# Attention sums stored with channels on partitions, denominators inverted once a head group and multiplied in by the row projection

## The chip, the cores and the metric

The kernel runs on one core of one Trainium2 chip. The metric is the device time of one execution in microseconds. The kernel before takes 2670.48 us, the median of 3 runs (2664.89 to 2671.22). The profiled execution took 2660.48 us, and its trace spans 2658.8 us.

## The reference, cut to what matters

One transformer block on x of shape 4 x 2048 x 256 (B, T, C), in float32. H = 16 heads of DH = 16 channels.

```python
def attention(x):                     # x: the layer-normed input
    q, k, v = heads(x)                # each (b, 16, 2048, 16), latent projections folded in, rotary on half
    scores = einsum('bhqd,bhkd->bhqk', q, k) / sqrt(16)
    att = softmax(where(causal, scores, -inf), axis=-1)
    y = einsum('bhqk,bhkd->bhqd', att, v)
    return y.transpose(0, 2, 1, 3).reshape(b, t, c) @ Wc

x = x + attention(layernorm(x))
z = layernorm(x).reshape(-1, 256)
gate = top-2 of 8 experts by z @ Wr + br, softmax over the two
x = x + sum over experts of gate * (relu(z @ W1 + b1) @ W2 + b2)
```

The softmax's denominator is the same for all 16 channels of a head and query. The kernel computes it as a 17th channel: the values have a column of ones, so the sum of the unnormalised exponentials comes out beside the 16 sums of values.

## The kernel before, in words

Four stages follow each other, each its own block of engine programs: `project` (queries, keys and values, written to HBM), `attend`, `mix` (the output projection Wc, the residual, the layer norm, the routing), and `experts`. The change touches `attend` and `mix`.

**attend** works through NG = 16 groups, a group w being one batch and GH = 4 heads (b = w // 4). Two streams share TensorE (PE):
- the maxima: PE computes scores with queries on partitions (L1004) into one of two PSUM slots `ps_m`, and VectorE (DVE) takes row maxima from it (L888 for whole blocks of keys, L892 on the diagonal). A ring counter (`plan_with_ring`) gives the slots in turn; PE waits for `piece_taken` of two pieces ago. When 12 (or the last 4) query tiles are done, DVE reduces them ("chain", L907), PE turns them ("turn_max", L1011), DVE splits them in two parts (L917, L919), and SyncE's queue (SP) sends them through HBM into the rows of `q_st` (`place_minus`, L733, L739).
- the sums: PE computes scores with keys on partitions (L963), ScalarE (ACT) takes the exponential (L865, L861), GpSimd (POOL) masks the diagonal (L814), and PE sums (L984): four heads, 17 rows each at partitions 32 h, into one PSUM bank `ps_o` of 512 queries.

A group has NSTEP = 40 "sum" steps, one for each tile of 128 keys, in four chunks c of 512 queries: 4, 8, 12 and 16 steps, that is steps 0 to 3, 4 to 11, 12 to 23 and 24 to 39. After the last step of a chunk ACT copies `ps_o` to `out_sb[:, c, :]` (L871). Then comes the operation "turn_out", 64 times in all: PE transposes the four 128 x 128 pieces of `out_sb` into a slot of the `ps_m` ring (L1015), DVE inverts the 16 denominators of each token (L926), waits that the store of two chunks before has landed, and multiplies (L931) into `y_sb`, and SP stores that to `y_dram`, which has tokens as rows (L757). At the end of a group's last sum, SP loads the heads of group w + 3 (`load`: 13 DMAs at L716 and L724, 3.6 MB).

The order of everything in `attend` is written out beforehand by a planner in Python, `attention_plan`. It simulates the engines with fixed durations and picks at each point the ready kind that can start first, less its `HOLD`. Every engine's program goes through the same list PLAN: each of PE, ACT, DVE and SP executes, in that order and with its own waits, what falls to it. So an engine that waits in one entry does nothing of what lies behind it.

**mix** takes NB = 16 blocks of 512 tokens. Before: SP loads a block of `y_dram` (`load_y`, L1136), PE transposes it (`turn_y`, L1452), ACT copies the halves to `yt` (L1206), PE multiplies by Wc (`mix_heads`, L1467), DVE adds the residual (L1328), then follow layer norm, transposes of the normalised rows, the router (L1479), the choice of two experts on DVE, and counts. POOL writes each token's entry into the experts' lists by 128 indirect DMAs, 8 a block (L1189), as soon as DVE has made its slots (L1437). SP also loads x four blocks ahead, stores the rows, and brings in 1 MB of expert weights a block. `experts` starts when POOL's last entry is written. In row p and column j of a block, token 4 p + j is kept.

## Time and profile before

| | us |
|---|---|
| median of 3 runs (lowest, highest) | 2670.48 (2664.89, 2671.22) |
| the profiled execution's own time | 2660.48 |
| its span in the trace | 2658.8 |
| PE busy | 2356.7 (89%) |
| DVE busy | 2044.3 (77%) |
| ACT busy | 1581.8 (59%) |
| POOL busy | 824.5 (31%) |

Busy time is the time in which an engine executed something; for PE the ends are modelled. The share is that of the whole span, so it mixes stages: `attend` runs from about 258 to 1930 us, `mix` to about 2132 us, `experts` to the end. In the rows further down a form such as 128x512 is partitions by elements, "idle before" is time in which the engine did nothing before these instructions, and the name behind an arrow is what ended that time. SPq is the queue of DMA-issuing instructions on SyncE.

### The profile page before, as it was taken

What the parts mean: (1) busy time and instruction counts of PE and PEld (TensorE: products, weight loads), DVE (VectorE), ACT (ScalarE), POOL (GpSimd) and SP (SyncE); (2) the same over time, 40 slices, a digit from 0 to 9 for tenths busy, and PEclk for the clock granted to TensorE, in tenths of its full rate; (3) what the DMA queues carried; (4) which work ended last, traced back from release to release, by engine and by line L of the source; (5) the groups of instructions that cost most, each with busy time, mean ns of one, the idle gap of its engine ahead of it and who ended that gap; (6) DMA issues with size and microseconds to landing.
All of it is one profiled execution on the core that took longest, in us unless ns stands there. A gap on an engine that the chain in (4) does not pass through costs nothing. (4 is left out here: it accounts for less than half of the span.)

```text
span 2658.8 us, 48214 instructions
## 1 busy us (share of the span) xinstructions
PE 2356.7 (89%) x15842; PEld 1342.6 (50%) x15842; DVE 2044.3 (77%) x5000; ACT 1581.8 (59%) x2716; POOL 824.5 (31%) x1132
## 2 busy tenths in 40 slices
PE   6786699999999999999999999998879379999998
PEld 6675233333343333333333333333256168998897
DVE  3785988988989899888889988993068557777776
ACT  3663177776777777766777777777745234444443
POOL 1444021121122112112112112112137755566554
PEclk7998599999999999999999999999989689999999
DMA  3777824135045045044144144101099323333332
GB/s 136 260 267 222 118 45 76 41 60 119 30 63 89 28 65 89 28 64 76 42 63 74 45 65 73 45 8 31 21 296 281 115 89 114 107 105 109 111 110 71
DMA packets 147718, 256.02 MB, mean 96 GB/s; under 512 B 72968, under 2 KB 92042, under 8 KB 139157
## 3 DMA queue, kind: packets, MB, share of 16 engines
q1 hardware_dynamic: 114544, 164.96, 28.0%
q0 software_dynamic: 29904, 80.65, 9.2%
q10 hardware_dynamic: 3028, 7.33, 1.7%
q8 instruction: 135, 2.21, 0.4%
q14 instruction: 107, 0.87, 0.1%
HBM read 147.65 MB, written 107.76 MB: 96 GB/s over the span
## 5 line engine op out<-in xcount | busy, mean ns | idle before, releaser
L865 ACT ACTIVATE prob<-ps_s 128x512 f32<-128x512 f32 (+5 forms) x1620 | 1078.5, 714 | 464.8 <-PE ps_s L963 462.2
L888 DVE TENSOR_REDUCE maxes<-ps_m 128x2 f32<-128x1024 f32 x768 | 914.1, 1222 | 112.6 <-PE ps_m L1004 109.3
L963 PE MATMUL ps_s<-q_st,k_st 50*128 50x512 f32 (+3 forms) x2560 | 605.4, 409 | 78.9 <-ACT prob L865 56.9
L1004 PE MATMUL ps_m<-k_st,q_st 48*128 48x512 f32 (+3 forms) x2560 | 605.1, 444 | 75.2 <-DVE maxes L888 39.6
L814 POOL TENSOR_SCALAR_AFFINE_SELECT prob<-prob 128x256 f32<-128x256 f32 x512 | 203.2, 406 | 1341.8 <-ACT prob L865 1211.9
L984 PE MATMUL ps_o<-prob,v_sb 128*17 128x512 f32 (+3 forms) x5120 | 606.7, 547 | 1.4 <-ACT prob L865 0.7
L1004 PEld LDWEIGHTS ps_m<-k_st,q_st 48*128 48x128 f32 x2560 | 273.6, 192 | 531.2 <-DVE maxes L888 261.3
L892 DVE CUSTOM_DVE_ANT_0 junk<-ps_m,causal 128x128 f32<-128x128 f32 (+3 forms) x1024 | 453.0, 484 | 47.6 <-PE ps_m L1004 45.9
L963 PEld LDWEIGHTS ps_s<-q_st,k_st 50*128 50x128 f32 x2560 | 316.6, 188 | 299.9 <-ACT prob L865 222.0
L1741 ACT ACTIVATE h_hi<-ps_turned 128x512 fp32r<-128x512 f32 x142 | 84.9, 598 | 213.9 <-PE ps_turned L1856 212.4
L94 PE MATMUL ps_out<-experts_hi,h_lo 128*128 (+1 forms) x568 | 171.6, 302 | 0.1
L984 PEld LDWEIGHTS ps_o<-prob,v_sb 128*17 128x17 f32 x5120 | 86.5, 95 | 168.5 <-issue 138.4
L96 PE MATMUL ps_out<-experts_hi,h_hi 128*128 (+1 forms) x568 | 160.4, 282 | 0.0
L95 PE MATMUL ps_out<-experts_lo,h_hi 128*128 (+1 forms) x568 | 160.1, 282 | 0.0
L1189 POOL DMA_INDIRECT list_dram<-entry,slots x128 | 123.9, 968 | 76.2 <-issue 39.6
L1770 DVE TENSOR_TENSOR h<-ps_hidden,b_sb 128x512 f32<-128x512 f32 x142 | 98.3, 692 | 43.9 <-PE ps_hidden L96 43.4
L1784 DVE TENSOR_TENSOR y<-ps_out,b_sb 128x256 f32<-128x256 f32 x142 | 60.3, 425 | 87.0 <-PE ps_out L96 87.0
L94 PE MATMUL ps_hidden<-experts_hi,x_lo 128*128 (+1 forms) x284 | 125.5, 442 | 0.3 <-issue 0.2
L96 PE MATMUL ps_hidden<-experts_hi,x_hi 128*128 (+1 forms) x284 | 112.6, 396 | 0.0
L95 PE MATMUL ps_hidden<-experts_lo,x_hi 128*128 (+1 forms) x284 | 112.4, 396 | 0.0
L1731 ACT ACTIVATE xn<-rows,lists 128x256 f32<-128x256 f32 x142 | 84.0, 591 | 47.1 <-DMA rows<-rows_dram,lists 46.2
L95 PEld LDWEIGHTS ps_out<-experts_lo,h_hi 128*128 128x128 f32 x568 | 107.6, 189 | 0.1
(187 smaller groups left out, 3065.8 us busy)
## 6 DMA issues: line engine op xcount, KB each, us to landing
parts_dram<-parts SPq DMA_DIRECT2D x64, 512.0 KB, 3.8
q_st<-parts_dram SPq DMA_DIRECT2D x84, 256.0 KB, 8.9
k_st<-parts_dram SPq DMA_DIRECT2D x84, 256.0 KB, 18.2
v_dram<-v_out SPq DMA_DIRECT2D x16, 544.0 KB, 5.5
xin<-in_L_attn_x SPq DMA_DIRECT2D x16, 512.0 KB, 6.0
ffn_raw<-in_L_ffn_W POOLq DMA_DIRECT2D x32, 256.0 KB, 5.2
y_dram<-y_sb SPq DMA_DIRECT2D x64, 128.0 KB, 2.0
split_hi<-ffn_hi POOLq DMA_DIRECT2D x16, 512.0 KB, 3.2
```

The lines of the kernel that those rows point to most:

```text
L94: nc.tensor.matmul(out, s_lo, m_hi, start=first, stop=False, skip_group_check=True)
L95: nc.tensor.matmul(out, s_hi, m_lo, start=False, stop=False, skip_group_check=True)
L96: return nc.tensor.matmul(out, s_hi, m_hi, start=False, stop=last, skip_group_check=True)
L814: nc.gpsimd.affine_select(out=tile, in_=tile, compare_op=ALU.is_ge, fill=0.0, base=0, pattern=[[0, 2], [1, P]], channel_multiplier=-1).the ...
L865: last_exp = nc.scalar.activation(prob[:, at:at + n, lo:TB], bank[:, 0:n, lo:TB], ACT.Exp, scale=DH ** -0.5)
L888: return nc.vector.tensor_reduce(maxes[:, 2 * pair:2 * pair + 2, qt, kc], bank[:, :, :], AX.X, ALU.max)
L892: last = nc.vector.tensor_tensor_reduce(junk[:, slot, i, 0:w], bank[:, i, 0:w], causal[:, TB - w:TB], 1.0, NEG, ALU.add, ALU.max, maxes[:, ...
L963: mm = nc.tensor.matmul(ps_s[k % 2][:, i, lo:TB], k_st[half(h % 2, ROWS), w % BUFS, h // 2, kt * P:(kt + 1) * P], q_st[half(h % 2, ROWS), ...
L984: mm = nc.tensor.matmul(ps_o[32 * h:32 * h + VW, lo:TB], v_sb[:, w % BUFS, kt, h, :], prob[:, (s % PROBS) * GH + h, lo:TB], start=STEP_FIR ...
L1004: mm = nc.tensor.matmul(ps_m[slot][:, i, 0:wide], q_st[half(i, STACK), w % BUFS, pair, qt * P:(qt + 1) * P], k_st[half(i, STACK), w % BUFS ...
L1189: pool.indirect_dma_start(list_dram[:, :], bass.IndirectOffsetOnAxis(ap=slots[:, j, i:i + 1], axis=0), entry[:, j, i, :], None).then_inc(s ...
L1770: nc.vector.tensor_tensor(out=h[:, s % 2, :], in0=ps_h[s % 2][:, :], in1=b1_sb[:, bass.ds(e, 1), :].rearrange("p a n -> p (a n)"), op=ALU. ...
```

## The change

At the end of a chunk, SP stores `out_sb[:, c, :]` as it is, 128 partitions by 512 queries, 256 KB, into `y_dram`, which now has 32 rows a head (16 channels, the denominator, 15 unused) and tokens as columns. The 64 "turn_out" operations go, from the planner too. In the next group's steps, SP loads the group's denominators as 128 x 64 (at step 3), DVE inverts them (at step 12), SP stores them to `inverse_dram` (at step 20); the last group's are handled by ACT's queue and DVE at the start of `mix`. There `load_y` brings channels on partitions, `load_inverse` brings each head's inverse 16 times over, DVE multiplies the two into `yt` in the tile order (`scale_heads`), and the transposes and ACT's copies of y go. A constant table in `attend` is made by an iota instead of a load. Cut to its core:

```diff
-HOLD = {"max": -171, "scores": -140, "sum": 0, "turn_out": -266}
+HOLD = {"max": -171, "scores": -140, "sum": 0}
+HEAD_ROWS = 32
+INVERSE_LOAD, INVERSE_MADE, INVERSE_STORE = 3, 12, 20
...
-        if outs:
-            ready["turn_out"] = max(outs[0][1], taken[-SLOTS]) + 53
...
-        else:
-            plan.append(("turn_out", outs.pop(0)[0]))
-            tile_free[:], issued = [start + 430, start + 430], start + 430
-            vector = max(start + 630, vector - 85) + 700
-            taken.append(vector)
...
+        sums_v = y_dram.rearrange("(g r) n -> g r n", r=HEAD_ROWS)
...
+        def load_sums(eng, g, to, done):
+            eng.dma_start(to, sums_v[g % HG * GH:(g % HG + 1) * GH, DH,
+                          g // HG * T:(g // HG + 1) * T].rearrange("g (q n) -> g q n", n=T // HEAD_ROWS)
+                          ).then_inc(done, 16)
+
+        def store_inverse(eng, g, of, done):
+            eng.dma_start(inverse_dram[g % HG * GH:(g % HG + 1) * GH, g // HG * T:(g // HG + 1) * T].rearrange(
+                "g (q n) -> g q n", n=T // HEAD_ROWS), of).then_inc(done, 16)
...
-                elif e[0] == "turn_out":
-                    w, c = e[1] // CH, e[1] % CH
-                    sp.wait_ge(piece_taken, ring + 1)
-                    to = y_dram[(w // HG) * T + c * TB:(w // HG) * T + (c + 1) * TB,
-                                (w % HG) * (GH * DH):(w % HG + 1) * (GH * DH)]
-                    sp.dma_start(to.rearrange("(j p) n -> p j n", p=P),
-                                 y_sb[:, c % 2, :, :, :].rearrange("p j h d -> p j (h d)")
-                                 ).then_inc(y_stored[c % 2], 16)
-                elif e[0] == "sum" and (e[1] + 1) % NSTEP == 0 and (e[1] + 1) // NSTEP + BUFS - 1 < NG:
-
-                    sp.wait_ge(summed, e[1] + 1)
-                    load(sp, (e[1] + 1) // NSTEP + BUFS - 1)
-            for i in range(2):
-                sp.wait_ge(y_stored[i], 16 * (NG * CH // 2))
+                elif e[0] == "sum":
+                    w, c, _ = STEP_LIST[e[1]]
+                    step = e[1] % NSTEP
+                    if w and step == INVERSE_LOAD:
+
+                        for u in range(2):
+                            sp.wait_ge(y_stored[u], 32 * w)
+                        if w >= 3:
+                            sp.wait_ge(inverse_stored[(w - 1) % 2], 16 * ((w - 1) // 2))
+                        load_sums(sp, w - 1, inverse[:, (w - 1) % 2, :], sums_in)
+                    elif w and step == INVERSE_STORE:
+                        sp.wait_ge(inverse_made, w)
+                        store_inverse(sp, w - 1, inverse[:, (w - 1) % 2, :], inverse_stored[(w - 1) % 2])
+                    if STEP_LAST[e[1]]:
+
+                        sp.wait_ge(out_copied, w * CH + c + 1)
+                        sp.dma_start(y_dram[w % HG * P:(w % HG + 1) * P, w // HG * T + c * TB:w // HG * T + (c + 1) * TB],
+                                     out_sb[:, c, :]).then_inc(y_stored[c % 2], 16)
+                    if e[1] + 1 == (w + 1) * NSTEP and w + BUFS < NG:
+
+                        sp.wait_ge(summed, e[1] + 1)
+                        load(sp, w + BUFS)
+            for u in range(2):
+                sp.wait_ge(y_stored[u], 32 * NG)
+                sp.wait_ge(inverse_stored[u], 16 * len(range(u, NG - 1, 2)))
...
+                    w, c, _ = STEP_LIST[e[1]]
+                    if w and c < 2:
+                        act.wait_ge(y_stored[c], 32 * w)
                     act.wait_ge(summed, e[1] + 1)
-                    nc.scalar.copy(out_sb[:, STEP_LIST[e[1]][1], :], ps_o[:, :]).then_inc(out_copied, 1)
+                    nc.scalar.copy(out_sb[:, c, :], ps_o[:, :]).then_inc(out_copied, 1)
...
-                elif e[0] == "turn_out":
-                    c, made = e[1] % 2, e[1] // 2
-                    src = ps_m[slot][:, 0, :].rearrange("p (j h d) -> p j h d", j=TILES, h=GH)
-                    dve.wait_ge(piece_made, ring + 1)
-                    nc.vector.reciprocal(rec[:, c, :, :], src[:, :, :, DH]).then_inc(rec_made, 1)
-                    dve.wait_ge(rec_made, e[1] + 1)
-                    if made:
-
-                        dve.wait_ge(y_stored[c], 16 * made)
-                    nc.vector.tensor_tensor(out=y_sb[:, c, :, :, :], in0=src[:, :, :, 0:DH],
-                                            in1=rec[:, c, :, :].unsqueeze(3).broadcast_to([P, TILES, GH, DH]),
-                                            op=ALU.mult).then_inc(piece_taken, 1)
+                elif e[0] == "sum" and e[1] >= NSTEP and e[1] % NSTEP == INVERSE_MADE:
+                    w = e[1] // NSTEP - 1
+                    dve.wait_ge(sums_in, 16 * (w + 1))
+                    nc.vector.reciprocal(inverse[:, w % 2, :], inverse[:, w % 2, :]).then_inc(inverse_made, 1)
...
-                    else:
-                        pe.wait_ge(out_copied, e[1] + 1)
-                        for j in range(TILES):
-                            mm = nc.tensor.transpose(ps_m[slot][:, 0, j * P:(j + 1) * P],
-                                                     out_sb[:, e[1] % CH, j * P:(j + 1) * P], ident[:, :])
...
             def load_y(n):
-                sp.dma_start(y_in[:, n % YB, :, :], y_v[n, :, :, :]).then_inc(y_loaded[n % YB], 16)
+                tokens = slice(n * TB, (n + 1) * TB)
+                for a in range(CC):
+                    sp.dma_start(y_in[:, n % YB, a, :],
+                                 y_v[a * HP:(a + 1) * HP, 0:DH, tokens]).then_inc(y_loaded[n % YB], 16)
+
+            def load_inverse(n):
+                if n == NB - CH:
+                    sp.wait_ge(inverse_stored[(NG - 1) % 2], 16 * (NG // 2))
+                tokens = slice(n * TB, (n + 1) * TB)
+                for a in range(CC):
+                    sp.dma_start(inverse_in[:, n % 2, a, :],
+                                 inverse_dram[a * HP:(a + 1) * HP, tokens].unsqueeze(1).broadcast_to([HP, DH, TB])
+                                 ).then_inc(y_loaded[n % YB], 16)
...
                 if n + YB < NB:
-                    sp.wait_ge(rows_turned, units(n, False) + 2)
+                    sp.wait_ge(y_scaled, n + 1)
                     load_y(n + YB)
+                if n + 2 < NB:
+                    sp.wait_ge(y_scaled, n + 1)
+                    load_inverse(n + 2)
...
+            act.dma_start(inverse[:, :],
+                          y_v[(HG - 1) * GH:HG * GH, DH, (B - 1) * T:B * T].rearrange(
+                              "g (q n) -> g q n", n=T // HEAD_ROWS)).then_inc(sums_in, 16)
...
-            copy_turned(yt)
             act.wait_ge(weights_in, 3 * 16)
             for n in range(NB + 2):
                 if n == 0:
-                    act.wait_ge(mixed, 2)
-                    copy_turned(yt)
+                    act.wait_ge(inverse_made, NG)
+                    act.dma_start(inverse_dram[(HG - 1) * GH:HG * GH, (B - 1) * T:B * T].rearrange(
+                        "g (q n) -> g q n", n=T // HEAD_ROWS), inverse[:, :]
+                                  ).then_inc(inverse_stored[(NG - 1) % 2], 16)
...
+            def scale_heads(n):
+                dve.wait_ge(y_loaded[n % YB], 32 * CC * (n // YB + 1))
+                if n:
+                    dve.wait_ge(mixed, 2 * n)
+                tt(out=yt[:, :, :, :], in0=y_in[:, n % YB, :, :].rearrange("p a (q j) -> p a j q", j=TILES),
+                   in1=inverse_in[:, n % 2, :, :].rearrange("p a (q j) -> p a j q", j=TILES),
+                   op=ALU.mult).then_inc(y_scaled, 1)
+
+            scale_heads(0)
+            dve.wait_ge(sums_in, 16 * NG)
+            nc.vector.reciprocal(inverse[:, :], inverse[:, :]).then_inc(inverse_made, 1)
+            scale_heads(1)
...
+                if n + 2 < NB:
+                    scale_heads(n + 2)
                 if m >= 0:
...
-            def turn_y(n):
-                pe.wait_ge(y_loaded[n % YB], 16 * (n // YB + 1))
-                turn(y_in[:, n % YB, :, :])
...
-                pe.wait_ge(turned_copied, units(n, False) + 2)
+                pe.wait_ge(y_scaled, n + 1)
...
-                                                yt[:, a, j * P:(j + 1) * P], wc_sb[:, a, :],
+                                                yt[:, a, j, :], wc_sb[:, a, :],
...
-    y_dram = nc.dram_tensor("y_dram", (B * T, C), F32).ap()
+    y_dram = nc.dram_tensor("y_dram", (H * HEAD_ROWS, B * T), F32).ap()
+    inverse_dram = nc.dram_tensor("inverse_dram", (H, B * T), F32).ap()
```

What is left out is declarations, arguments, the semaphores that are passed from `attend` to `mix`, waits whose counts follow from the removed transposes, and the iota.

## Rows read from the trace of the kernel before

**Rows 1.** Windows of attend: start:end, length, busy us by engine, PEclk, DMA share, GB/s.
```profile
400.00:1816.00 1416.00, 1314.67 (x9322) 547.96 (x9324) 1258.11 (x2730) 1024.41 (x1630) 263.22 (x534) 0.98 0.33 59
1816.00:1931.00 115.00, 93.84 (x592) 30.50 (x591) 7.12 (x19) 86.91 (x137) 18.01 (x39) 0.98 0.06 16
```

**Rows 2.** Groups by line, whole span: busy us, mean ns of one, idle before.
```profile
L1015 PE MATMUL ps_m<-ident,out_sb 128*128 128x128 f32 x256 | 42.2, 288 | 9.3 <-DVE maxes L888 4.9 <-DVE maxes L892 1.5 <-ACT out_sb L871 1.4
...
L931 DVE TENSOR_TENSOR y_sb<-ps_m,rec 128x256 f32<-128x256 f32 x64 | 27.2, 424 | 4.7 <-DMA y_dram<-y_sb 2.6
...
L926 DVE RECIPROCAL rec<-ps_m 128x16 f32<-128x16 f32 x64 | 16.2, 254 | 112.0 <-PE ps_m L1015 111.1
```

**Rows 3.** Timeline of PE around one turn_out: start us, us, instruction.
```profile
1093.81 0.66 PE L1015 MATMUL ps_m<-ident,out_sb 128*128 128x128 f32 x4
1094.39 0.53 PE L1004 MATMUL ps_m<-k_st,q_st 48*128 48x512 f32 x2
```

**Rows 4.** Timeline of SP's queue at the start of group 8.
```profile
1131.79 2.83 SPq L716 DMA_DIRECT2D q_st<-parts_dram  x6
...
1138.60 0.43 SPq L733 DMA_DIRECT2D minus_dram<-minus_rows  x1
1161.86 1.23 SPq L739 DMA_DIRECT2D q_st<-minus_dram  x2
```

**Rows 5.** The y_dram store behind the load of 930.14 us: start, and landing.
```profile
L757 SPq DMA_DIRECT2D y_dram<-y_sb x1: 432/432/432, 936.1 to 936.1; - x1
...
DMA to landing us min/median/max: 23.0/23.0/23.0
```

**Rows 6.** Timeline of ACT: group's end and next chunk 1's end, twice.
```profile
426.63 0.59 ACT L871 COPY out_sb<-ps_o 128x512 f32<-128x512 f32 x1
...
457.23 0.59 ACT L871 COPY out_sb<-ps_o 128x512 f32<-128x512 f32 x1
...
1637.58 0.59 ACT L871 COPY out_sb<-ps_o 128x512 f32<-128x512 f32 x1
...
1666.99 0.59 ACT L871 COPY out_sb<-ps_o 128x512 f32<-128x512 f32 x1
```

**Rows 7.** Timeline of DVE and PE around step 12 of group 8.
```profile
1160.56 2.36 DVE L888 TENSOR_REDUCE maxes<-ps_m 128x2 f32<-128x1024 f32 x2 [0.31 <-PE ps_m L1004]
...
1165.24 0.42 DVE L931 TENSOR_TENSOR y_sb<-ps_m,rec 128x256 f32<-128x256 f32 x1 [2.16 <-DMA y_dram<-y_sb]
...
1165.72 0.50 PE L1004 MATMUL ps_m<-k_st,q_st 48*128 48x512 f32 x2 [2.42 <-DVE y_sb L931]
```

**Rows 8.** Timeline of all engines: end of attend, start of mix.
```profile
1925.79 0.58 ACT L871 COPY out_sb<-ps_o 128x512 f32<-128x512 f32 x1 [1.17 <-PE ps_o L984]
...
1927.92 0.36 SPq L757 DMA_DIRECT2D y_dram<-y_sb  x1
1930.35 0.36 ACTq L1199 DMA_DIRECT2D numbers<-in_tile_numbers  x1
```

**Rows 9.** Timeline of POOL in mix: first and last of 128 list writes.
```profile
1966.69 1.05 POOL L1189 DMA_INDIRECT list_dram<-entry,slots  x1 [34.80 <-DVE slots L1437]
...
2130.96 0.97 POOL L1189 DMA_INDIRECT list_dram<-entry,slots  x1 [0.31 <-issue]
```

**Rows 10.** Windows: one block of mix (columns as in Rows 1).
```profile
2021.50:2030.30 8.80, 8.03 (x55) 5.76 (x55) 7.34 (x48) 5.02 (x11) 6.76 (x7) 1.00 0.99 275
```

**Rows 11.** DMA of mix, 2003 to 2056 us, and its main queue.
```profile
DMA packets 4632, 15.24 MB, mean 288 GB/s; under 512 B 1753, under 2 KB 1753, under 8 KB 3818
...
q1 hardware_dynamic: 3230, 15.07, 98.3%
```

**Rows 12.** Timeline of all engines: the first product with Wc.
```profile
1938.54 5.41 PEld L1467 LDWEIGHTS ps_x<-wc_sb,yt 128*128 128x128 f32 x16 [2.49 <-DMA br_sb<-in_L_ffn_br]
```

**Rows 13.** Groups by line: DVE tensor_tensor of 512 elements, from PSUM and from SBUF.
```profile
L1328 DVE TENSOR_TENSOR x<-ps_x,x_own 128x512 f32<-128x512 f32 x16 | 10.4, 687 | 7.9 <-PE ps_x L1467 7.2 <-DMA rows_dram<-x 0.6
...
L378 DVE TENSOR_TENSOR turned<-raw,cos 128x512 f32<-128x512 f32 x32 | 28.9, 904 | 0.0
```

More of the change, by code:

```diff
@@ L519, in attention_plan @@
     taken, exp_end = [0.0] * SLOTS, [0.0] * 2
-    outs, exp_done, masked, rows = [], [], {}, {}
+    exp_done, masked, rows = [], {}, {}
     k = s = at = 0
@@ L593, in attention_plan @@
             k += 1
-        elif kind == "sum":
+        else:
             plan.append(("sum", s))
@@ L703, in plan_with_ring @@
                 yield e, ring
-                ring += e[0] in ("max", "turn_max", "turn_out")
+                ring += e[0] in ("max", "turn_max")
         def turn_number(w, late):
@@ L1029, with mix @@
 XB = 4
-def mix(nc, x, y_dram, wc, wr, br, split_dram, tile_numbers, w_sb, b1, b2, biases, biases_in, block, slots_made, scattered, numbers, run, entry, slots, rows_dram,
+def mix(nc, inverse_done, x, y_dram, inverse_dram, wc, wr, br, split_dram, tile_numbers, w_sb, b1, b2, biases, biases_in, block, slots_made, scattered, numbers, run, entry, slots, rows_dram,
         pairs_dram, list_dram):
```

94 lines of the change are left out of this document (40 added, 54 removed).

## The prediction

> **What bounds the kernel now.** I read the windows by stage first. In `attend`, from 400 to 1816 us, PE is busy 1314.7 of 1416 us (93%) and DVE 1258.1 (89%); ACT has 72%, and DMA a third [rows 1]. So two engines share the bound there: PE feeds DVE through a ring of two slots, and what is taken from only one of them is half a gain. From 1816 us on the maxima are done, DVE is idle, and PE and ACT alternate. By the ACT copies that end its groups, one group of heads takes about 100 us. The stage's end is a chain: last copy, transposes, division, store, landing, next stage [rows 8]. In `mix` the timeline of POOL shows 128 list writes that hardly stop from 1966.69 to 2130.96 us, 1.29 us each, 10.3 us a block, after 34.8 us of idling until the first slots [rows 9]. PE and DVE go through a block in 8.8 us, with 8.0 and 7.3 us of work [rows 10]. So `mix` lasts until the first slots are made, and then 128 writes, as long as later slots come at most 10.3 us apart. `experts` isn't touched and starts when POOL is done. The profiled execution (2660.48 us) lies 10.0 us below the median of the timed runs; the sum is made against it, and the difference then carried to the median.
>
> **The transposes and divisions that go.** One turn_out holds PE from 1093.81 until the next product at 1094.39 us, 0.58 us [rows 3]; over the 62 that I followed in PE's timeline the median is 0.585 us. On DVE it takes 0.254 + 0.424 us [rows 2]. Both engines of the bound are relieved, by 2.3 and 2.7 us of a group's 100, in nearly the share that each has, so I take PE's time in full: 63 x 0.585 = 36.9 us less (the 64th is the end, below). At least 25 us (the four behind 1816 us lie half beside ACT, and waits elsewhere in the ring may grow), at most 46 us (with the idle time before them, 9.3 us [rows 2]). ACT's copy (0.59 us) stays.
>
> **The end of attend.** Now the copy ends at 1926.37, the store is issued at 1927.92, and `mix` begins at 1930.35 us [rows 8]. The store will be issued 1.5 us earlier; it is 256 KB instead of 128, for which I take 0.4 us off: 1.1 us less (0.5 to 1.5).
>
> **The new wait, in the middle of DVE's program.** DVE waits at step 12 for the denominators of the group before. Behind it stand all further maxima, and behind these, through the two slots, PE with both streams. When does DVE get there, and when is the load there?
> - The load is issued by SP at step 3. SP doesn't wait for that step itself, but the 13 DMAs for group w + 3 stand before it in the same queue, issued at the group's start, in 13 groups. What is issued behind them lands after them. In group 8 SP stores the parts of the maxima at 1138.60 and goes on only at 1161.86 us, 30.1 us after the load began [rows 4]. In group 6 a store of y issued at 936.1 lands 23.0 us later, 29.0 us after the load began at 930.14 [rows 5]. I take 29.5 us for the mean. In the new order SP first waits for the copy (0.6 us), issues the y store (0.4 us) and has its 256 KB ahead (0.9 us at the 288 GB/s of [rows 11]; I take it at 1 us), so the denominators land 31.5 us after the group's last sum.
> - DVE gets to step 12 just after chunk 1 ends. Its copy comes 30.6 us after the group's start in group 1 and 29.4 us in group 13 [rows 6]; the mean of the 13 groups is 29.6 us, 27.7 to 33.0. DVE still has the pieces made before the step: in group 8 until 1162.92 us, 31.0 us after the start [rows 7]. I take 31.2 us for the mean, less 1.2 us for the two turn_outs that go: 30.0 us.
>
> So DVE stands still for 1.5 us, and the reciprocal of 64 columns comes on top. The trace has it for 16 columns, 0.254 us [rows 2]; between that and four times it, 1.0 us, I take 0.4 us. What does PE lose? There is a precedent: in group 8 DVE waited 2.16 us in a turn_out for a store behind the same load, and PE stood for 2.42 us [rows 7]. There one of the two slots was held by the turn_out itself; here PE can still fill both, which lets it go on for about 1.1 us more (a piece takes DVE 1.2 us). That gives 1.9 - 1.1 = 0.8, taken as 0.9 us, in 10 groups: 9 us. In the other 3 (groups 6 to 8, by where L733 comes in SP's timeline) `place_minus` lies between the group's load and step 3. There SP sleeps until its own store has landed (31.5 us), issues two DMAs (1.23 us [rows 4]), and only then the load (0.4 us), which lands 2.0 us later: 35.1 us. DVE stands for 5.1 us, and PE loses 5.1 + 0.4 - 1.1 = 4.4 us: 13 us for three. Together 22 us more. In groups 14 and 15 nothing is in the queue. Bounds: 0, and 51 us (DVE there 1.2 us earlier and no free slots: 10 x 3.1 + 3 x 6.7). The inverse's store at step 20 and the waits of ACT are for things long landed: nothing, and at worst 0.4 us a group.
>
> Beside this stands a rule of the Trainium skill (DMA: Bandwidth & Descriptors, section "Queues, rings and completion order"): each DMA engine takes descriptors in ring order, but a transfer is spread over up to 16 rings and completion isn't first in, first out for an issuing engine. By that rule a small later load could land before the large one is through, and the 22 us would be 0; the trace speaks against it, 23.0 us for 128 KB [rows 5]. It is the first rival below.
>
> **mix.** Removed: 8 transposes a block (0.9 us of PE) and two copies of ACT, which weren't the bound. Added: `scale_heads` on DVE, 1024 elements from SBUF. A tensor_tensor of 512 takes 0.687 us from PSUM and 0.904 us from SBUF beside a working POOL [rows 13], so twice that, 1.37 to 1.81 us, less one instruction's start: I take 1.3 us. It stands just before the wait for the counts, where DVE idles for about 1 us, so the block stays at 9 to 9.5 us, under POOL's 10.3. It costs only before the first slots: two of them in full, 2.6 us, less two turns of y that PE no longer does (1.8 us). Before the first product with Wc, which starts at 1938.54 us, released by the last of the weights [rows 12], two inverses are now queued, 1.05 MB: 3.6 us at 288 GB/s [rows 11]. Together 4.4 us later. Then the DMA: a block moves 2.62 MB now (y, x and rows 0.52 each, weights 1.05) and 3.15 MB with the inverse. The queue is 98.3% busy at 288 GB/s already [rows 11], so 10.9 us a block, 0.6 us more than POOL needs, in the seven or so blocks after the first ones; the lead over POOL of the first blocks covers that, and I add nothing. Bounds for the stage: 2 us less (all of the start hidden) to 15 us more (2 KB rows move at 260 GB/s, 12.1 us a block).
>
> **Sum.** -36.9 - 1.1 + 22 + 4.4 = -11.6 us: 2648.9 us for a profiled execution like the one shown, and from the median 2670.5 - 11.6 = 2659 us.
>
> **The rivals.**
> - The wait costs nothing: the denominators land before DVE asks. For it: expected standstill is only 1.5 us in ten groups, a difference of two numbers near 30. Against: what lands behind the load [rows 4, 5], and that the removal brings DVE there sooner. -36.9 - 1.1 + 4.4 = -33.6: 2637 us.
> - Slower: in every group with a load the order is as in groups 6 to 8, or DVE gets to step 12 some 3 us sooner than I take it, so that each of 13 groups loses 4.4 us: 57 us, and -33.6 + 57 = +23.6: 2694 us. It decides from 2.6 us a group on (33.6 / 13). For it: the precedent shows DVE's wait passed on to PE in full [rows 7], and the planner, which doesn't know of this wait, may move the maxima. Against: `place_minus` comes later than step 12 or before the load in ten groups.
> - `mix` becomes bound by its DMA: slots then come 12 us apart and not 10.3, 15 us in place of 4.4: 2670 us, no difference. For it: 98.3% [rows 11]. Against: the first and last blocks move less.
>
> **How the numbers follow.** Forecast 0.50, wait hidden 0.22, slower 0.15, DMA-bound `mix` 0.13. What a measurement can tell from no change is 0.3%, 8 us, here 2662.5 to 2678.5. The forecast's own range is 2646 to 2672, and two thirds of it are faster by that much. Faster 0.34 + 0.22 + 0.01 = 0.57; same 0.14 + 0.02 + 0.10 = 0.26; slower 0.02 + 0.13 + 0.02 = 0.17. The range of 2634 to 2685 takes in the hidden wait and most of the way to the slower case.
>
> **What would show each step.** The windows: PE's busy time from 400 us to the end of the maxima down by about 40 us, DVE's by as much. The waits of DVE: a row of the reciprocal waiting for the `inverse` load, 13 times, some 15 + 15 us in total, the longest near 5 us, and as much idle time of PE before L1004. POOL's first list write 41 us after the start of `mix` (36.3 before), and the writes without gaps. Wrong would be: no such wait (then 2637), or one of over 3.7 us in each group (2.6 us of PE and the slots' 1.1), or gaps between POOL's writes.

## The result, and the profile after

The changed kernel takes **2745.6 us** (median of 4 runs, 2734.28 to 2755.40) beside 2670.85 us of the kernel before on the same chip: 1.028 times as long, interval 1.0234 to 1.0327. Forecast were 2659 us, and 2634 to 2685 with 8 chances in 10. Here and below medians are over all runs of a kernel, while ratios and intervals leave out runs that lie over 1.5% above its shortest. The profiled execution took 2734.28 us with a span of 2732.5 us, 73.7 us more than that of before (2658.8). By stage the 73.7 us are:

| | before | after | difference |
|---|---|---|---|
| start to last copy of `attend` | 1925.79 | 1927.87 | +2.1 |
| last copy to POOL's first list write | 40.9 | 67.9 | +27.0 |
| first to last list write | 164.3 | 207.0 | +42.7 |
| last list write to the end | 527.8 | 529.7 | +1.9 |

The timelines of after at the two borders (start us, us, instruction, idle before and its releaser) answer to [rows 8] and [rows 9]:

```profile
1927.87 0.59 ACT L883 COPY out_sb<-ps_o 128x512 f32<-128x512 f32 x1 [1.17 <-PE ps_o L988]
1928.48 0.32 SPq L769 DMA_DIRECT2D y_dram<-out_sb  x1
1931.05 0.35 ACTq L1210 DMA_DIRECT2D numbers<-in_tile_numbers  x1
...
1995.81 1.07 POOL L1200 DMA_INDIRECT list_dram<-entry,slots  x1 [63.20 <-DVE slots L1464]
...
2202.81 0.97 POOL L1200 DMA_INDIRECT list_dram<-entry,slots  x1 [0.30 <-issue]
```

POOL waited 34.80 us for its first slots and then hardly again; now it waits 63.20 us, and 42.7 us more in eleven gaps. The groups by line of `mix` show what makes the slots late (behind the second bar stands the idle time before them, and what ended it):

```profile
L1200 POOL DMA_INDIRECT list_dram<-entry,slots x128 | 126.6, 989 | 144.6 <-DVE slots L1464 105.9 <-issue 38.7
L1490 PE MATMUL ps_x<-wc_sb,yt 128*128 128x256 f32 x256 | 83.2, 496 | 72.9 <-DVE x L1353 54.7 <-DMA br_sb<-in_L_ffn_br 18.2
L1335 DVE TENSOR_TENSOR yt<-b_sb,inverse_in 128x1024 f32<-128x1024 f32 x16 | 31.8, 1987 | 79.8 <-DMA inverse_in<-inverse_dram 66.6 <-PE ps_x L1490 13.2
```

**One block of `mix`**, block n + 2's inverses followed from SP's queue to their use, with the windows behind it (columns as in [rows 1]: busy us of PE, PEld, DVE, ACT and POOL, then PEclk, DMA share and GB/s):

```profile
2012.76 2.75 SPq L1140 DMA_DIRECT2D inverse_in<-inverse_dram  x2
...
2027.44 6.05 SPq L1140 DMA_DIRECT2D inverse_in<-inverse_dram  x2
...
2035.56 1.97 DVE L1335 TENSOR_TENSOR yt<-b_sb,inverse_in 128x1024 f32<-128x1024 f32 x1 [6.80 <-DMA inverse_in<-inverse_dram]
```
```profile
2014.00:2017.00 3.00, 2.61 (x27) 1.39 (x24) 0.19 (x2) 1.07 (x2) 2.39 (x3) 1.00 0.93 341
2017.00:2020.00 3.00, 0.91 (x6) 0.32 (x4) 0.49 (x1) 2.46 (x5) 1.13 (x2) 0.93 0.57 141
2028.00:2031.00 3.00, 2.61 (x28) 1.72 (x27) 0.72 (x7) 1.07 (x2) 2.18 (x3) 1.00 1.23 299
2031.00:2034.00 3.00, 1.36 (x7) 0.34 (x5) 0.00 (x0) 2.01 (x4) 1.70 (x2) 1.00 0.54 166
2034.00:2037.00 3.00, 0.00 (x0) 0.00 (x0) 1.44 (x1) 0.64 (x2) 0.00 (x0) 0.94 0.51 183
2037.00:2040.00 3.00, 0.40 (x1) 0.43 (x2) 2.54 (x9) 0.00 (x0) 0.85 (x1) 0.50 0.45 148
```

The inverses issued at 2012.76 us are used at 2035.56: 22.8 us. VectorE stands still for the last 6.8 us of them while the DMA share is **0.5**, at 166 to 183 GB/s, though SP has more loads waiting (its issue at 2027.44 takes 6.05 us, where an unhindered pair takes 1.2). In the kernel before the share was 1.02 at 284 GB/s over the whole stretch of 1990 to 2060 us:

```profile
1990.00:2060.00 70.00, 63.84 (x432) 45.70 (x431) 57.90 (x368) 39.98 (x80) 53.22 (x56) 1.00 1.02 284
```

Cut into windows of 1 us, the share lies between 0.40 and 0.65 in 3% of them there and in 49% of those of after (44% from 1990 to 2130 us). About half of what the 16 DMA engines could do goes unused while loads are waiting; that it is half of the engines is shown under "What halves the share". In the chain of work that ended last, the landing of the inverses takes 42.1% of 1927 to 2203 us. PE's granted clock is lower in `mix` as well, 0.82 from 1995 to 2060 us where it was 1.00; a product with Wc takes 496 ns on average for 395.

**attend.** The windows answer to [rows 1], then come the two stretches at the end:

```profile
400.00:1816.00 1416.00, 1303.27 (x9166) 531.50 (x9164) 1231.92 (x2641) 1035.55 (x1644) 264.72 (x535) 0.97 0.34 66
...
1830.00:1880.00 50.00, 45.19 (x201) 12.74 (x198) 0.00 (x0) 28.88 (x48) 6.07 (x16) 0.54 0.03 12
...
1880.00:1930.00 50.00, 39.10 (x241) 11.73 (x237) 0.00 (x0) 38.04 (x57) 7.98 (x12) 1.00 0.09 32
```

The last maxima are done at 1783.62 us in place of 1818.97, 35.4 us earlier. But the last group, which has no maxima beside it, takes 107.8 us (1820.08 to 1927.87) in place of 91.6: PE's granted clock is at its lower level (0.5 is 1.2 of 2.4 GHz) for most of 1820 to 1880 us, 0.54 on average from 1830 to 1880. In that window it was at 0.97 before:

```profile
1830.00:1880.00 50.00, 42.74 (x279) 14.88 (x278) 2.05 (x6) 38.87 (x68) 9.54 (x24) 0.97 0.04 9
```

One other group is long, the one that begins at 826.61 us, with 114.0 us:

```profile
833.22 0.42 SPq L716 DMA_DIRECT2D v_sb<-v_dram  x1
833.68 0.43 SPq L734 DMA_DIRECT2D minus_dram<-minus_rows  x1
856.36 1.23 SPq L740 DMA_DIRECT2D q_st<-minus_dram  x2
857.71 0.57 SPq L721 DMA_DIRECT2D inverse<-y_dram  x1
...
860.13 0.55 DVE L937 RECIPROCAL inverse<-inverse 128x64 f32<-128x64 f32 x1 [4.58 <-DMA inverse<-y_dram]
...
861.10 0.79 PE L1008 MATMUL ps_m<-k_st,q_st 48*128 48x512 f32 x2 [4.81 <-DVE maxes L904]
...
870.00:890.00 20.00, 19.55 (x78) 6.93 (x78) 12.45 (x20) 9.63 (x14) 0.00 (x0) 0.50 0.00 1
```

Here `place_minus` lies between the group's load and the load of the denominators, as the prediction described for groups 6 to 8. SP goes on only at 856.36, VectorE waits 4.58 us and PE 4.81, and then PE's clock is at 0.50 for some 32 us more, until 893 us.

### The profile page after: what moved, and what is told of

Its sections match the earlier page's. It is cut to its first block and busy times, and to the rows that moved or that the text cites. A ratio compares the mean times of both kernels' runs of the same rounds, so it can differ in the third digit from the quotient of the medians.

```text
span 2732.5 us, 47304 instructions
## 1 busy us (share of the span) xinstructions
PE 2361.3 (86%) x15458; PEld 1331.4 (49%) x15458; DVE 2039.9 (75%) x4904; ACT 1565.7 (57%) x2684; POOL 828.7 (30%) x1132
## 5 line engine op out<-in xcount | busy, mean ns | idle before, releaser
L967 PE MATMUL ps_s<-q_st,k_st 50*128 50x512 f32 (+3 forms) x2560 | 616.4, 414 | 78.5 <-ACT prob L874 53.1
L988 PE MATMUL ps_o<-prob,v_sb 128*17 128x512 f32 (+3 forms) x5120 | 623.8, 560 | 1.8 <-ACT prob L874 0.7
L967 PEld LDWEIGHTS ps_s<-q_st,k_st 50*128 50x128 f32 x2560 | 323.8, 193 | 303.1 <-ACT prob L874 223.4
L1490 PE MATMUL ps_x<-wc_sb,yt 128*128 128x256 f32 x256 | 83.2, 496 | 72.9 <-DVE x L1353 54.7
L95 PE MATMUL ps_hidden<-experts_lo,x_hi 128*128 (+1 forms) x284 | 112.8, 397 | 0.0
```

The source lines that it names most:

```text
L95: nc.tensor.matmul(out, s_hi, m_lo, start=False, stop=False, skip_group_check=True)
L967: mm = nc.tensor.matmul(ps_s[k % 2][:, i, lo:TB], k_st[half(h % 2, ROWS), w % BUFS, h // 2, kt * P:(kt + 1) * P], q_st[half(h % 2, ROWS), ...
L988: mm = nc.tensor.matmul(ps_o[32 * h:32 * h + VW, lo:TB], v_sb[:, w % BUFS, kt, h, :], prob[:, (s % PROBS) * GH + h, lo:TB], start=STEP_FIR ...
```

## The experiments

They ran on five chips. On one of them (c_before, c_after, e7, e5) the kernel before takes 2671 us, as in the first measurement; on the other four 2733 to 2735 us. Stage times are therefore compared within a kind of chip: the longer kind has c2_before and c2_after. "Stage" is from the last copy of `attend` to the last list write, 205.2 us in the first trace of before and 274.9 in that of after. "Group" is a group of heads.

**Twice the two kernels again.** The kernel before:

> The kernel before, unchanged, for its trace on this chip: on the chip of the first experiments its time was 2734 us and not 2670, and the experiments' traces show there small idle times of VectorE and ScalarE that the two first traces don't have. If they belong to the chip this run shows them too, in `mix` above all; if they belong to the change (loads of y in rows of 2 KB) this run has none.

c_before: 2673.1 us (ratio 1.0006, 0.9971 to 1.0040), stage 205.7 us, without the idle times. The changed one:

> The changed kernel, unchanged, on the same chip as the others of this call. Expected 1.02 to 1.035 times the kernel before, with the loss in `mix` (block to block 14 us and more in place of 8.8 us), whatever the chip.

2734.16 us, ratio 1.0209 (1.0127 to 1.0290), stage 277.2 us, blocks 12.8 us apart on average from the fourth on (8.8 before). c2_before and c2_after, on a longer chip:

> The kernel before for its trace on this chip. The chips of the first and third call took 2735 us for it, the second 2671. On one of the first kind its `mix` and its experts should show the same small idle times of VectorE and ScalarE that all experiments there show: mix 230 to 250 us in place of 205, experts 22 us longer. If they don't, these idle times belong to the experiments' code.

> The changed kernel for its trace on this chip: mix 275 us from last copy to last list write on a chip of the second kind, 290 to 320 on one of the first, if the inverses' loads are late there as well; last group of attend 105 to 118 us.

c2_before has those idle times: they come with the chip and not with the change. Stage 245.6 us, its blocks 13.3 us apart from the fourth on. c2_after: 2768.54 us, ratio 1.0115 (1.0072 to 1.0158), stage 279.1 us, less than the 290 to 320 expected. So the longer chip hides part of the change's cost: +33.5 us for the stage there, +71.5 on c_before's.

**e7: no scaling, no inverses.** Edit in `mix`:

```diff
-                scale_heads(n + 2)                 # and (0), (1), and all load_inverse
-                pe.wait_ge(y_scaled, n + 1)
+                pe.wait_ge(y_loaded[n % YB], 16 * CC * (n // YB + 1))
-                    yt[:, a, j, :], wc_sb[:, a, :]
+                    y_in[:, n % YB, a, :].rearrange("p (q j) -> p j q", j=TILES)[:, j, :], wc_sb[:, a, :]
```

> Left out in `mix`: the scaling and the loads of the inverses; TensorE takes its weights straight from y as loaded (rows of 2 KB, every fourth column). What is left of the change in `mix` is the layout of y, and it has 8 transposes and two copies of ScalarE a block less than before. Theory (the scaling on VectorE's path, with the inverses' loads behind it, costs what `mix` lost): blocks at 8.8 us or less, the slots ready before POOL wants them, 40 to 75 us under the changed kernel, at or below the kernel before (0.985 to 1.0 of it). Rival (y's rows of 2 KB, 256 descriptors a block, or weights read with a stride of 16 bytes): still above 1.01.

2680.82 us, ratio 0.9992 (0.9950 to 1.0034). Stage 1948.40 to 2160.24 = 211.8 us: 65 of the 71.5 us are gone with the multiplication and the inverses' loads together, and 6 stay, nearly all at the start (the first block's rows are stored 24.7 us after the last copy, 19.5 before). Nothing was won below the kernel before, since `attend` ended at 1948.40 us (1932.81 in c_before). The stage's two ends in e7:

```profile
1948.40 0.59 ACT L883 COPY out_sb<-ps_o 128x512 f32<-128x512 f32 x1 [1.17 <-PE ps_o L988]
...
2160.24 0.97 POOL L1196 DMA_INDIRECT list_dram<-entry,slots  x1 [0.30 <-issue]
```

**Which of the two: loads or multiplication?** e1, and k2 with the reciprocal moved as in e5 (g1 and h2 have the same `mix`), drop `load_inverse(n + 2)`, so that 14 blocks are scaled with the inverses of the first two; k3 adds such loads to the kernel before:

```diff
+            def load_extra(n):                     # k3: into buffers of its own, read by nobody
+                for a in range(CC):
...
+                    sp.dma_start(extra[:, n % 2, a, :],
+                                 y_rows[row:row + HP, :].unsqueeze(1).broadcast_to([HP, DH, TB])
```

> Left out: in `mix` the inverses are loaded for blocks 0 and 1 only, and the other 14 blocks are scaled with those two; everything else is the changed kernel's. In the changed kernel `mix` takes 272 us up to the last list write and 201 us in the kernel before; VectorE waits 66.6 us in it for the inverses. Theory (the loads of the inverses, 512 KB a block, are what holds the blocks back): blocks come every 10.3 us again, and the time falls by 60 to 70 us, to 2675 to 2685 us. Rival 1 (the loads of y, now 256 rows of 2 KB in place of 128 of 4 KB, are the slow ones, with the issue time that they take on SP): 2725 us or more. Rival 2 (the multiplication of 1.97 us and TensorE's lower clock set the pace): 2735 to 2745.

> The changed kernel (reciprocal at step 24) with the loads of the inverses left out from block 2 on, the multiplication kept. On a fast chip: the changed kernel's stage takes 275 us (e5: 266), the one without scaling and loads 212. If the loads hold the blocks: 215 to 225 us and a time of 2680 to 2690. If the multiplication on VectorE does: 250 and more, 2715 and more. On a slow chip 263 to 266 us, as in three runs there, against 246 of the kernel before: 16 of the 17 in the first four blocks.

> The kernel before with nothing but the loads added: in `mix`, per block, the same two DMAs of 256 KB with 2 KB rows, each read 16 times over, at the same places in SyncE's program, into two buffers of their own that nobody reads. Stage from the last copy of `attend` to the last list write: 205 us in the kernel before on a chip where it takes 2671 us, 246 on one where it takes 2735 (c2_before). If the bytes alone load the queue so that y, x and the weights come late, the stage grows by 30 us or more and the first product with Wc starts 6 us later; if the loads cost only because VectorE has to wait for them, the stage grows by less than 15 us (some 6 of them at the start).

All on longer chips, beside 245.6 us of before and 279.1 of after. Timelines of c2_before, k3 and k2, last copy and last list write:

```profile
1943.80 0.58 ACT L871 COPY out_sb<-ps_o 128x512 f32<-128x512 f32 x1 [1.17 <-PE ps_o L984]
...
2189.37 0.97 POOL L1189 DMA_INDIRECT list_dram<-entry,slots  x1 [0.30 <-issue]
```
```profile
1942.01 0.58 ACT L871 COPY out_sb<-ps_o 128x512 f32<-128x512 f32 x1 [1.17 <-PE ps_o L984]
...
2198.07 0.96 POOL L1207 DMA_INDIRECT list_dram<-entry,slots  x1 [0.30 <-issue]
```
```profile
1939.80 0.59 ACT L883 COPY out_sb<-ps_o 128x512 f32<-128x512 f32 x1 [2.03 <-PE ps_o L988]
...
2201.22 0.97 POOL L1198 DMA_INDIRECT list_dram<-entry,slots  x1 [0.30 <-issue]
```

k3: 256.1 us, +10.5 (2743.89 us, ratio 1.0033, 1.0010 to 1.0056). k2: 261.4, +15.8 (2741.64 us, ratio 1.0014, 0.9984 to 1.0044); e1 265.7 (2757.74 us, ratio 1.0068, 1.0034 to 1.0102), g1 265.1, h2 262.8. Neither is "the" cause: loads alone cost 10, and the new y, the multiplication and two inverses 16 to 20. That adds up to 26 to 31 of the 33.5 us, with the first two inverses counted in both, so a part comes only when both are there. The start splits well. The first rows are stored 19.4 us after the last copy in c2_before; y's new layout adds 5 (e7), the loads of two inverses 7.7 (k3), and the changed kernel has 32.7. From the first stored rows to the fourth, c2_before and k3 take 22.4 us, k2 26.1 and c2_after 35.3: here the two together cost 12.9 us where the loads alone cost nothing. Later the blocks of k3 and k2 come 13.5 and 13.2 us apart, those of before 13.3 and of c2_after 13.9: such a chip hides there most of what the other shows.

**Late because asked for late?** e2 was to have four buffers for the inverses, but its tiles don't fit in SBUF (one needs 2048 bytes where 1888 are left), so it has no time. g3 has three buffers in place of two, g4 issues the loads from ScalarE's queue, e3 reads 128 different rows in place of 8 rows 16 times (g3 and g4 also have the reciprocal of `attend` at step 24):

> The changed kernel with the reciprocal at step 24, and three buffers for the inverses in place of two, so that each is asked for three blocks ahead; same bytes. In the changed kernel VectorE waits 66 us for them in 13 blocks, up to 8 us each. If they are late because they are asked for late (behind 2.1 MB of x, rows and weights), the waits nearly go, blocks come every 10 to 11 us and the time is 2680 to 2695. If the queue can't carry the bytes or the descriptors, blocks stay at 13 us or more, and the time at 2715 to 2735.

> The changed kernel with the reciprocal at step 24, and the inverses from block 2 on loaded by ScalarE's queue, so not behind SyncE's x, rows and weights; two buffers as before, same bytes. If it was the place in the queue, the inverses land in 4 us or so, blocks come every 10 to 11 us: 2680 to 2700. If it is the sum of bytes or descriptors on the 16 engines, no more than 10 us are won: 2715 to 2735.

> The changed kernel, but the second operand of the multiplication is loaded from y's own rows (128 different rows of 2 KB) in place of 8 rows of the inverses read 16 times each; so y is squared and nothing is divided. Same bytes, same descriptors' size, same places in the queue. If reading one DRAM row 16 times over is what is slow, the time falls to 2680 to 2700 us; if it is the bytes, the descriptors or the place in the queue, it stays at 2735 to 2755.

2757.89 us (1.0077, 1.0043 to 1.0112), 2775.83 (1.0139, 1.0079 to 1.0199) and 2768.44 (1.0119, 1.0054 to 1.0183); stages 280.9, 293.3 and 286.2 us, none under 279.1. All three ran on chips of the longer kind. VectorE's wait for the inverses, c2_after and then g3:

```profile
DVE yt L1335 <- DMA inverse_in<-inverse_dram: 37.8, 8, 7.5
```
```profile
DVE yt L1337 <- DMA inverse_in<-inverse_dram: 16.6, 4, 7.6
```

The wait was halved and the stage didn't shrink. So on these chips neither an earlier request nor another queue nor distinct rows bring the time back. On a chip of the first kind none of the three was tried. In all three the half share is there (42, 34 and 42% of the 1 us windows of 1990 to 2130 us).

**A version with few bytes.** e4 loads the inverses as 16 rows and lets PE spread them; g2 and h1 add the filling below, k1 puts two small weights first (these three have the reciprocal at step 24):

```diff
-                                 inverse_dram[a * HP:(a + 1) * HP, tokens].unsqueeze(1).broadcast_to([HP, DH, TB])
+                sp.dma_start(inverse_in[:, n % YB, :], inverse_dram[0:H, tokens])      # 32 KB
+                    last = nc.tensor.matmul(ps_s[a][:, :], spread[:, a * P:(a + 1) * P], inverse_in[:, n % YB, :])
```

> A version meant to keep the gain of `attend`: the inverses are loaded as they are, 16 rows of 2 KB (32 KB) a block, four blocks ahead, and TensorE spreads them over the 256 channels with two products of a 0/1 matrix (0.65 us each), in place of the eight transposes of y (0.9 us) that the kernel before had; VectorE multiplies from PSUM in two instructions of 0.69 us. If the loads of the inverses are what holds `mix` back: its blocks come every 10.3 us, the stage takes 205 us like that of the kernel before, and the time is that of attend's balance, 2665 to 2685 us. If y's rows of 2 KB or the multiplication are the cause it stays above 2725.

> Candidate without filling: reciprocal at step 24, inverses as 16 rows spread by TensorE, and the two small weights' loads (Wr, br) put first in `mix`, ahead of y(0), so that the first product with Wc no longer waits for what lands behind 1 MB. It starts 8.2 us after the stage's first instruction in the kernel before, 20.5 in the changed one, 13.9 without the inverses; here 9 to 12 expected. On a fast chip stage 208 to 215 us and 2665 to 2680, the same as the kernel before within 0.4%; on a slow one 270 us (275.9 to 279.1 without the new order) and 1.010 times the kernel before.

Stages 277.4 (e4), 279.1 (g2), 275.9 (h1), 276.1 us (k1), against 245.6; e4 2771.27 us (1.0134, 1.0086 to 1.0181), k1 2760.97 (1.0086, 1.0059 to 1.0114). The first product of k1 starts 13.1 us after the stage's first instruction, not 9 to 12. Fewer bytes didn't help here, but the version doesn't single them out: y still comes at half share (20% of the windows in h1, 22% in k1), PE has two products of 512 columns more in the round of each block, and the transposes have two PSUM banks for three. No version beat the kernel before.

**attend: the reciprocal later.**

```diff
-INVERSE_LOAD, INVERSE_MADE, INVERSE_STORE = 3, 12, 20
+INVERSE_LOAD, INVERSE_MADE, INVERSE_STORE = 3, 24, 32
```

> The changed kernel with the reciprocal moved from step 12 to step 24 of 40 and the inverse's store from step 20 to step 32; `mix` as in the changed kernel. In its trace VectorE waited 4.58 us for the denominators in the group that begins at 826.6 us, TensorE stood for 4.81 us, and its granted clock was 0.50 for the next 30 us; that group took 114 us where the others take 97.5. Theory (that wait costs 16 us by the clock): no such wait, no group over 105 us but the last and the one with the prefill, and 10 to 18 us less than the changed kernel. Rival (the clock falls there anyway, as it falls once or twice in the traces of both kernels): within 5 us of the changed kernel.

2726.1 us beside 2734.16 of c_after (1.0213 and 1.0209 of before, intervals 0.017 wide, so the times alone don't tell). The traces do, since the edit is in nine kernels. Group 5 (counted from 0, the one of 826.61 us) takes 97.0 to 98.3 us in eight of them and 103.5 to 114.0 in the seven with step 12; in the four of before it takes 98.8 to 111.1. The 14 groups behind group 0, which ends at 427 us, take 1406.2 us on average with step 12 (7 traces, 1393.7 to 1418.2), 1391.8 with step 24 (the eight traces without h2's, 1382.8 to 1400.0), and 1415.8 with the transposes (4 traces, 1407.5 to 1426.8). On one chip the same: 1406.7 and 1412.9 in c_after and e7, 1382.8 in e5. So step 12 cost some 14 us. VectorE's waits for the denominators add to 5.8 us in after (4.58 once, 1.2 in three others), to 2.1 to 7.8 us in the seven traces, and to nothing with step 24. The rest fits the lower clock behind them: from the stop on, group 5 of after has it for 34 us, those with step 24 for 3 to 7 us.

**attend: the tail.** Four transposes that nobody reads at each chunk's end (g1), two before each pair of scores (g2), one (h1, h2):

> Three edits on the changed kernel: the reciprocal at step 24 and the store at step 32; four transposes of the identity matrix, read by nobody, on TensorE at the end of each chunk of sums once all maxima are done (the places where the kernel before had its turn_outs; about five times); and, left out, the loads of the inverses from block 2 on. Tail: in all seven traces with the new `attend` the last group took 107.8 to 117.9 us at a granted clock of 0.5 for 50 us and more, in the two of the kernel before 91.6 and 96.0. If TensorE's clock fell there because the transposes no longer fill the gap at a chunk's end, the last group is back at 92 to 98 us; if not, 107 or more. Mix: the multiplication of 1.97 us on VectorE is still there, only the loads are missing. If the loads are the cause, last copy to last list write takes 206 to 215 us, as in the run without the scaling (212); if the place of the multiplication in VectorE's program is, over 240. Time with both: 2655 to 2670.

> Candidate: the reciprocal at step 24; two transposes of the identity matrix before every pair of scores in the tail, four at a chunk's end; and the inverses loaded as 16 rows and spread by TensorE. If the 232 us that this `mix` took before were of that chip, it takes 205 to 215 us here. Tail: last group 92 to 100 us if filling TensorE's idle time holds its clock; the filling may cost up to 8 us where it isn't idle. Time 2650 to 2670, below the kernel before by up to 20 us; if `mix` is bound by the block's round through VectorE and TensorE, 2700 and more.

> Candidate again (reciprocal at step 24, inverses as 16 rows spread by TensorE), with half the filling: one transpose of the identity matrix before each pair of scores in the tail, two at a chunk's end. Tail: with two before each pair the granted clock stayed 1.00 there, but TensorE was busy throughout and the last group took 117.1 us; with one, about 10 us of work go into some 14 us of idle time. If idle time is what takes the clock away, and one is enough: last group 94 to 102 us at 1.00; else 105 and more. Mix, on a chip whose kernel before takes 2671: 205 to 215 us from last copy to last list write if the inverses' bytes were the cause; on one where it takes 2735, compared with that chip's own trace of the kernel before: no more than 12 us above it.

> The same `attend` as in h1_fill1_spread (for a second look at its tail), with the changed kernel's `mix` from which the loads of the inverses are left out from block 2 on. If the loads are what holds the changed kernel's blocks, the stage is within 12 us of the kernel before on the same chip; if the multiplication of 1.97 us on VectorE does, it is 25 us and more above it.

Last group: 112.5 us (g1), 117.1 (g2), 107.2 (h1). Twelve traces without filling have 104.2 to 118.0, mean 112.8; the four of before 91.6 to 96.0, mean 93.6. The lower clock goes with it: PE has it for 44 to 82 us of that group in the twelve (104.2 us with 44, 107.8 with 55, 118.0 with 82), and for 3 to 17 us in the four. That is 3.7 us of the group for each 10 us at the lower clock, so the clock accounts for the whole growth, by an estimate from these traces. In g2 and h1 it is at 1.00 throughout, but PE is then busy nearly all the time. The windows of h1, and of h2 with the same `attend`:

```profile
1830.00:1880.00 50.00, 48.80 (x272) 18.46 (x271) 0.00 (x0) 35.88 (x56) 5.46 (x14) 1.00 0.03 12
```
```profile
1830.00:1880.00 50.00, 49.52 (x216) 16.90 (x208) 0.00 (x0) 26.37 (x42) 4.69 (x12) 0.69 0.02 6
1880.00:1930.00 50.00, 50.00 (x165) 15.76 (x164) 0.00 (x0) 22.45 (x33) 8.00 (x12) 0.50 0.07 27
```

So filling costs what it wins. Whether idle time is what takes the clock away there stays open. g2 and h1 agree with it; in h2's trace the clock fell to 0.50 with PE busy all the time, and the last group took 155.8 us, but that execution took 2787.23 us where the same kernel took 2733.10 at the shortest, so nothing is built on it. g1 was 2739.79 us (1.0013, 0.9984 to 1.0042), g2 2773.87 (1.0135, 1.0089 to 1.0182). h1 and h2 had runs of up to 2852.87 us; their times are not compared.

## Why the prediction was wrong

The steps that failed are the two terms for `mix`: +4.4 us for its start, where 27.0 were measured, and nothing for blocks that were to stay under POOL's 10.3 us, where POOL's gaps took 42.7 us. Both priced the new loads by their bytes at 288 GB/s, and the traces show them at half that share of the engines. Beside them the gain in `attend` was taken for the stage's time and came to nothing. The rival "`mix` becomes bound by its DMA" had the right place with a fifth of the price, 15 us for the stage. The numbers by step:

- **Transposes and divisions, -36.9 us.** Right for the stream that they shared: the last maxima end 35.4 us earlier. Mis-sized as time: the median group fell from 100.3 to 98.0 us, but the 14 groups behind group 0 together only by 9.7 us on average (24.0 with the late reciprocal), and the last group grew by 19 us. I took PE's time as the stage's time, and gave the last group no term at all. The sums behind the last maxima go on at 92 us a group at best, so maxima that end earlier buy little. Why PE's clock is at its lower level for 44 us and more of that group in all twelve unfilled traces, and for 17 at most in the four of before, stays open.
- **The end of attend, -1.1 us.** Copy to store 0.61 us (2.13 before), store to stage 2.57 (2.43): 1.4 us less, right.
- **The wait at step 12, +22 us.** Mechanism right, size too large: 10 groups were to stand 1.5 us each, three stood 0.3 to 0.6 and the others not at all; three were to stand 5.1 us, one stood 4.58. In the trace of after `place_minus` stands between the group's load and step 3 in group 5 alone, since the maxima get ahead faster; I had read groups 6 to 8 off the old order. What I had left out is the clock after a stop of 4.8 us. By e5's comparison 14 us.
- **The rule of the Trainium skill on completion order** (DMA: Bandwidth & Descriptors, "Queues, rings and completion order"), by which the small load could have landed before the large one. In group 1 the load was issued at 433.52 us, behind the large load, and VectorE got the denominators at 457.3, 30.9 us after the group's end (31.5 taken): the trace again spoke for landing behind the load.
- **The start of mix, +4.4 us.** This failed: 27.0 us. The first product starts 20.5 us after the stage's first instruction (1951.55, released by `br_sb`) and not 8.2 [rows 12]; I had 3.6 us for it:

```profile
1937.49 2.46 SPq L1158 DMA_DIRECT2D wr_sb<-in_L_ffn_Wr  x1
1939.99 1.60 SPq L1159 DMA_DIRECT2D br_sb<-in_L_ffn_br  x1
...
1951.55 5.27 PE L1490 MATMUL ps_x<-wc_sb,yt 128*128 128x256 f32 x16 [18.24 <-DMA br_sb<-in_L_ffn_br]
```
  Half of the 12.3 us is SP, which issues `br_sb` 8.9 us into the stage (2.3 before): 11 DMAs stand ahead of it for 5, and the later issues take longer (2.46 and 1.60 us for 0.45 and 0.37). The other half is landing, 11.6 us for 5.8. Then the first blocks come 12 us apart, where they came 5.8 us apart twice: 13.8 us more up to the fourth.
- **The block under POOL's 10.3 us, +0.** This failed: 42.7 us of gaps between POOL's writes, the third of the signs by which the prediction was to be known as wrong. I put all bytes at 288 GB/s. By the windows above the 1.05 MB of y and inverses move at about 170 GB/s, at half share: 6.2 us, and the other 2.1 MB take 7.3 us at 288 [rows 11]: 13.5 us a block, an estimate from rows. Measured are 13.1 from the fourth block to the last ((226.1 - 68.4) / 12). My bound of 260 GB/s for rows of 2 KB came from no row and was no bound at all: in 2031 to 2037 us the rate was 166 to 183.
- **The multiplication, 1.3 us.** It takes 1.97 us, above the 1.81 that I had worked out, and the reciprocal 0.549 (0.4 taken). `yt` also has one buffer, so it waits for the product of the block ahead (13.2 us in two waits at the start).

**What halves the share.** The packets in the traces show which loads do it. In the kernel before, from 1930 to 2120 us, 16 packets are in flight at once for 49% of the time and 8 for 1%; in after, from 1931 to 2190 us, 16 for 27% and 8 for 20%. Nearly all packets of 2048 bytes there are y's and the inverses' (the kernel before has none): at most 12 of them are in flight at once, and more than 8 in 4% of the time that any is, while larger packets reach 19. An engine seems to have about one packet in flight, since 16 go with a share of 1.0. So the new loads run on some 8 of the 16 engines and the others on all. The Trainium skill has a rule for it, on the same page from which I took the other one (DMA: Bandwidth & Descriptors, "Rules for kernel authors"): the number of engines is set by the slowest dimension, other than 1, of the access patterns, and an outermost dimension under 16 confines the whole DMA to at most that many. The sources of both new loads begin with HP = 8 heads; by the page that is at most 8 engines, and the trace agrees with its share of 0.51 and its 8 packets in flight. y was [128, ...] before. I had read the page for a wait and not held the new loads against it. What the confinement costs by itself is argued, not shown: no run here has the outer dimension changed to 16 or more. With y alone on 8 engines, e7's stage is 6 us longer than before, and that of k3, with the inverses' loads of the same shape (16% of the 1 us windows of 2010 to 2150 us at half share), 10.5 us. Nor was the split between loads and multiplication tried on a chip of the first kind.

## What to carry to other kernels

Hold every new DMA against two numbers in the trace after it, its share of the engines and its GB/s: a share that stands at one half with loads waiting points at the loads' shape, and a byte count at the mean rate missed it here. When work is taken off two streams that share an engine, ask which of them ends last: here the maxima ended 35 us earlier and `attend` did not. A wait that stops TensorE costs more than its length when the clock falls behind it; 4.8 us cost a group some 12 us more here.

## What the runs showed of the hardware

- Two kinds of chip for the same kernel, 2671 and 2733 to 2735 us. Of the difference 40 us lie in the stage behind `attend` (245.6 for 205.2 us) and 20 in `experts` (548 for 528). On the longer kind VectorE, once POOL writes its lists, has idle times between instructions that depend only on each other (0.55 us before a reciprocal of its own result) and others with no releaser in the profile (c2_before):

```profile
DVE place L1426 <- remote: 30.8, 9, 5.3
...
2047.73 0.18 DVE L1404 RECIPROCAL share<-whole 128x4 f32<-128x4 f32 x1 [0.55 <-DVE whole L1399]
```
- The last group of `attend` took 3.7 us more for each 10 us at the lower clock (104.2 us with 44 us of it, 118.0 with 82).
- Packets in flight tell how many DMA engines a load uses: the loads whose source begins with 8 heads stay at about 8, the others reach 16 and more.
- A pair of DMAs that SP issues in 1.2 us took 6.05 us at 2027.44 us, behind loads that had not landed.
- A multiplication of 1024 elements a partition whose operands are read in steps of four elements took 1.97 us; two of 512, one operand from PSUM, 1.05 us each (k1), where a plain 512 from PSUM takes 0.687 [rows 13].
